# A four-layer kernel on one core: another order for the parts of all five engines, and PSUM banks taken from a table

## The reference, cut to what matters

```
x = x + attn0(xn, 16 heads, causal, alibi) + rms_norm(silu(xn @ G0) * (xn @ U0)) @ D0   # G0, U0, D0 ternary
x = x + recurrence1(xn) + experts1(xn, top 2 of 16, at most 128 rows each) + shared1(xn)
x = x + softmax((xn @ Wq) @ (xn @ Wk).T / 16) @ (xn @ Wv) @ Wo + (silu(xn @ G2) * (xn @ U2)) @ D2   # spline weights
x = x + attn3(xn, 16 heads, rotary) + (xn + shared3(xn) + experts3(xn, top 2 of 8, bf16))
```

## Time and profile before

| | |
|---|---|
| Median of 3 runs | 1509.37 us (1507.64 to 1509.67) |
| Span of the profiled execution, first to last instruction | 1501.9 us |
| Time around the span, by the median | 7.5 us |
| Instructions | 19,793 |
| Mean granted TensorE clock | 0.908 |
| HBM read, written | 44.03 MB, 10.52 MB |

### The profile page before, as it was taken

The page is one execution under the profiler, slowest core; times in us unless marked ns, Lnnn a source line. Parts: engine busy times, 40 slices in busy tenths (PEclk is TensorE's granted clock), DMA queues, the critical chain, the costliest instruction groups (busy, mean ns, idle before and its releaser), DMA issues.

```text
span 1501.9 us, 19793 instructions
## 1 busy us (share of the span) xinstructions
PE 1244.3 (83%) x7757; PEld 809.6 (54%) x7772; DVE 976.6 (65%) x1840; ACT 668.8 (45%) x967; POOL 420.9 (28%) x402
## 2 busy tenths in 40 slices
PE   0579999999998695889568999997887888788887
PEld 0358776667654352445246988874335345335333
DVE  6986457666648999974488345378546676756660
ACT  3344554655566664543114134231661553463462
POOL 3464440033003133121564123241222301401300
PEclk9979989999999897999569999997889899989988
DMA  7000000002210000044441000004001000100100
GB/s 226 23 1 1 1 2 2 1 2 92 87 46 29 0 29 28 1 138 140 149 67 28 1 1 1 8 18 105 1 1 57 1 0 21 37 1 1 57 0 15
DMA packets 31437, 53.26 MB, mean 35 GB/s; under 512 B 4880, under 2 KB 19440, under 8 KB 30576
## 3 DMA queue, kind: packets, MB, share of 16 engines
q1 hardware_dynamic: 27264, 41.02, 8.7%
q0 software_dynamic: 4080, 10.97, 3.4%
HBM read 44.03 MB, written 10.52 MB: 36 GB/s over the span
## 4 chain that ended last, share of the span: by engine, by line
PE 33%; DVE 22%; issue 6%; ACT 5%; POOL 2%; DMA 1%; SPq 0%; DVEq 0%; POOLq 0%
PE pair L617 11%; PE bank L617 11%; DVE max L1113 4%; PE bank L705 3%; ACT probs L1620 3%; PE pair L673 2%; PE pair L693 2%; POOL inbox L1967 1%; DVE conv L1194 1%; PE pair L655 1%; DVE xn L1032 1%; DVE sin L1081 1%; DVE x L1412 1%; DVE normed L1286 1%; DVE mix_h L1517 1%
## 5 line engine op out<-in xcount | busy, mean ns | idle before, releaser
L1113 DVE TENSOR_REDUCE max<-pair 128x2 f32<-128x1024 f32 (+3 forms) x256 | 250.8, 1019 | 90.4 <-PE pair L673 54.5
L1620 ACT ACTIVATE probs<-pair 128x1024 f32<-128x1024 f32 (+3 forms) x256 | 208.7, 871 | 106.0 <-PE pair L663 65.7
L673 PE MATMUL pair<-ks,qs 50*128 50x512 f32 (+3 forms) x512 | 115.9, 484 | 36.5 <-DVE max L1113 17.4
L705 PE MATMUL bank<-probs,v 128*32 128x512 f32 (+3 forms) x1024 | 127.3, 572 | 5.0 <-ACT probs L1620 4.8
L693 PE MATMUL pair<-qs,ks 52*128 52x512 f32 (+3 forms) x512 | 104.3, 454 | 24.9 <-DVE max L1113 4.5
L1933 POOL TENSOR_TENSOR h_low<-hidden,h_high 128x512 fp32r<-128x512 f32 x64 | 82.4, 1291 | 151.9 <-ACT h_high L1655 151.8
L693 PEld LDWEIGHTS pair<-qs,ks 52*128 52x128 f32 x512 | 47.9, 197 | 109.0 <-issue 36.0
L673 PEld LDWEIGHTS pair<-ks,qs 50*128 50x128 f32 x512 | 53.4, 210 | 88.9 <-DVE max L1113 35.2
L1993 POOL TENSOR_TENSOR h<-mix_h,h 128x512 bf16<-128x512 f32 x48 | 55.4, 1165 | 149.9 <-DVE mix_h L1517 108.5
L1146 DVE TENSOR_TENSOR x<-bank,x 128x512 f32<-128x512 f32 x32 | 22.0, 689 | 105.7 <-PE bank L617 102.2
L1163 DVE SCALAR_TENSOR_TENSOR hidden<-hidden,pair 128x512 f32<-128x512 f32 x64 | 43.8, 684 | 62.8 <-ACT hidden L1647 62.8
(11 more groups left out here) (334 smaller groups left out, 3002.1 us busy)
## 6 DMA issues: line engine op xcount, KB each, us to landing
expert_in<-in_experts_in SPq DMA_DIRECT2D x16, 352.0 KB, 4.1
expert_out<-in_experts_out SPq DMA_DIRECT2D x16, 256.0 KB, 4.9
h<-comb SPq DMA_DIRECT2D x4, 1024.0 KB, 5.8
x<-in_x SPq DMA_DIRECT2D x4, 512.0 KB, 8.2
tern_raw<-in_ffn_in SPq DMA_DIRECT2D x8, 256.0 KB, 6.3
inbox<-zeros SPq DMA_DIRECT2D x4, 512.0 KB, 5.2
tokens<-inbox SPq DMA_DIRECT2D x16, 128.0 KB, 2.3
outbox<-expert_y SPq DMA_DIRECT2D x16, 128.0 KB, 3.4
```

Source lines behind the costliest of these rows:

```text
L673: made = mm(to[:, hh, 0:n], m.qs[g % 2][r0:r0 + AUG + 2, p, qt * P:(qt + 1) * P], m.ks[g % 2][r0:r0 + AUG + 2, p, 0:n], start=True, stop=k ...
L705: made = mm(to[32 * j:32 * j + 32, q0:T], m.v[b % 2][:, kt, G * g + j, :], m.probs[(2 * kt + j // 2) % 4][:, j % 2, q0:T], start=kt == 0, ...
L1113: V.tensor_reduce(m.max[:, g % 2, qt, 2 * p:2 * p + 2], to[:, :, 0:n], AX.X, ALU.max).then_inc(*s.done("top"))
L1620: A.activation(m.probs[(2 * kt + p) % 4][:, :, q0:T], to[:, :, q0:T], ACT.Exp, scale=0.25).then_inc(*s.done("exp"))
```

## The change

`DUE` is replaced for all five engines: every part gets another number. The parts, their instructions and their waits for data and buffers stay as they are. On PE a part moves by 3.6 places on average (35 at most), on DVE by 9.7 (129), on ACT by 2.2 (59), on POOL by 4.9 (62), on SP by 3.3 (16). The number at place n of a name's line belongs to the n-th part of that name. The SP names of `load` are, in this order: ident, x0, bias0, qkv0, x1, x2, x3, extra0, wo0, inbox, small1, vec1, front1, gates1, rest1, qkv2, small3, bias3, qkv3, wo3, shared3.

The rotation of the banks is replaced by `TAKEN`, a table that gives for every PE part its first bank. A part that took a pair still takes one of the same three, and one that took a single bank takes 6 or 7; `weigh` and the parts that had bank 7 for themselves now share both. The waits for a bank's last readers are set as before, for the user that the table gives.

```diff
...
-    "tern_scaled": "4 11 6 8 16 14 15 27 18 29 33 30",
+    "tern_scaled": "5 8 12 11 13 15 16 21 19 20 27 24",
...
-    "stat": "2 1 3 5 13 22 21 24 23 45 25 50 47 48 49 51 161 160 156 163 217 218 223 224 298 300 302 304 346 344 345 347 524 534 533 540 543 554 555 558 570 562 563 572 587 585 586 592 606 607 610 611 636 637 642 643 670 671 666 673 722 723 697 724",
+    "stat": "2 1 3 4 36 38 37 39 71 61 68 72 74 93 104 106 171 172 213 220 224 235 233 251 296 309 321 326 359 379 362 394 525 533 528 534 561 559 555 562 587 594 593 601 597 596 595 600 628 629 622 654 651 652 642 662 688 687 689 690 778 771 774 833",
...
-    "norm": "7 10 12 9 41 44 42 38 57 55 54 56 81 78 79 80 168 169 167 166 231 236 235 232 361 375 360 363 393 391 389 392 547 548 549 546 566 568 569 567 584 577 582 583 601 603 599 600 630 633 631 629 662 661 659 663 694 690 692 691 781 780 778 779",
+    "norm": "7 6 9 10 41 42 48 45 91 83 94 86 195 207 186 120 240 227 237 244 320 262 322 306 350 353 347 355 405 404 406 409 538 539 536 537 566 572 573 567 605 604 606 611 635 636 641 631 655 656 664 676 679 683 670 743 821 764 785 766 893 880 894 896",
...
-    "split_high": "1 499 589",
+    "split_high": "5 558 588",
...
-    "split_low": "2 161 199",
+    "split_low": "8 183 193",
...
-    "based": "8 24 30 41 173 184 196 221",
+    "based": "5 56 61 103 190 216 235 280",
...
-    "load": "1 7 6 0 5 2 8 4 9 17 23 24 33 34 35 76 3 81 82 83 84",
+    "load": "1 2 10 9 15 6 18 13 21 22 23 29 28 32 33 78 19 81 82 85 83",
...
-    "tern_load": "11 13 12 10 14 15 16 18 21 19 20 22",
+    "tern_load": "0 3 5 4 8 7 12 11 14 16 17 20",
...
-    "spline_load": "78 77 79 80",
+    "spline_load": "76 77 79 80",
...
-PLACES = {"pair": ((0, 1), (2, 3), (4, 5)), "acc": ((6,),), "one": ((7,),), "two": ((6,), (7,))}
 BANKS = {"tern_sum": "pair", "turn": "pair", "qkv": "pair", "fold": "pair", "score": "pair", "refold": "pair", "prob": "pair", "weigh": "acc", "back": "one",
          "rows": "pair", "unit": "pair", "down": "one", "mean": "one", "proj": "pair", "gate": "two", "gamma": "pair", "inflow_turn": "pair", "mem_turn": "two",
          "shared": "pair", "count": "two", "expert_turn": "two", "expert_in": "pair", "expert_fold": "two", "expert_out": "two",
@@ -307,11 +306,46 @@
          "mix": "pair"}
 
 
-def bank_ring(name, key):
-    if name == "out":
-        return "one" if key[0] in HEADS else "two"
-    return BANKS[name]
-
+def width(name, key):
+    return 2 if BANKS.get(name) == "pair" else 1
+
+
+
+TAKEN = {name: [int(bank) for bank in banks] for name, banks in {
...
+    "turn": "0040004240020004",
...
+    "weigh": "66667777666677777777666677776666777777776666777766667777666666667777666677776666777766667777666677776666777766667777666677776666",
+    "back": "77766766666767676776777676766676",
...
+    "out": "67667776676777767677767776767676",
...
+    "gamma": "2024",
...
+    "shared": "2040204242242400",
...
+}.items()}
 
 
 FREED = {
@@ -385,14 +419,9 @@
         self.pe, self.dve, self.act, self.pool, self.sp = (
             Engine(e, self.sem(n)) for e, n in ((nc.tensor, "pe_step"), (nc.vector, "dve_step"), (nc.scalar, "act_step"), (nc.gpsimd, "pool_step"), (nc.sync, "sp_step")))
         self.banks, held = {}, {}
-        rank = {}
+        first = {(name, key): bank for name, banks in TAKEN.items() for key, bank in zip(parts["PE"][name], banks)}
         for name, key in self.turns.order["PE"]:
-            ring = PLACES[bank_ring(name, key)]
-            n = rank.get(bank_ring(name, key), 0)
-            rank[bank_ring(name, key)] = n + 1
-            place = ring[n % len(ring)] if name != "weigh" or key[-1] == 0 else self.banks["weigh", key[:-1] + (0,)][0]
-            if name == "weigh" and key[-1] > 0:
-                rank[bank_ring(name, key)] = n
+            place = tuple(range(first[name, key], first[name, key] + width(name, key)))
             self.banks[name, key] = (place, [held[bank] for bank in place if bank in held])
             for bank in place:
                 held[bank] = (name, key)
```

More of the change, by code:

```diff
@@ L307 @@
          "mix": "pair"}
-def bank_ring(name, key):
-    if name == "out":
-        return "one" if key[0] in HEADS else "two"
-    return BANKS[name]
+def width(name, key):
+    return 2 if BANKS.get(name) == "pair" else 1
+TAKEN = {name: [int(bank) for bank in banks] for name, banks in {
+    "tern_sum": "024022442024",
+    "turn": "0040004240020004",
+    "qkv": "00402022240402444204400200422424",
+    "fold": "2020424204420402040442242442000200244040222004222004240242242440",
+    "score": "4224440242220402022444002044200242004042404440224440000024040442220440004420220440040424204244204024042240004404020044420042224024040042422002402442220022004402402000200402444042242004404220244422444240224004242440040224222024440002440244200204242402022442",
+    "refold": "42220222220004224000400220442042",
+    "prob": "4400402024042440204222400044042240200240222424240240200202422424240404204422202404422002404022024242222440424042024404402004400444020442000442402404204204222204224242044200004242042020440420420240024242020240404040000220420242200042422002042400040402044202",
+    "weigh": "66667777666677777777666677776666777777776666777766667777666666667777666677776666777766667777666677776666777766667777666677776666",
+    "back": "77766766666767676776777676766676",
+    "rows": "202424402204",
+    "out": "67667776676777767677767776767676",
+    "unit": "0224404020440420200404204002400240200442024240240424020420400224",
+    "down": "76676677",
+    "mean": "6766",
+    "proj": "4204244022422224",
+    "gate": "6767776666677667",
+    "gamma": "2024",
+    "inflow_turn": "4420",
+    "mem_turn": "76777676",
+    "shared": "2040204242242400",
+    "count": "6667",
+    "merge": "76",
+    "expert_turn": "7676777777667667",
+    "expert_in": "4020044240240442",
+    "expert_fold": "6667676776677666",
+    "expert_out": "6667766767767766",
+    "spline": "240420402042",
+    "qk2": "2024",
+    "v2": "76767676",
+    "score2": "6766667667666676",
+    "probs_turn": "7767767667777676",
+    "comb_turn": "6767",
+    "mix": "202024224424444224400204244000022200044020240244",
+}.items()}
 FREED = {
```

## The result

The changed kernel takes **1366.1 us** by the median of four executions, the kernel before 1508.5 us: ratio 0.907, 95% interval 0.903 to 0.911. One of the four executions of the changed kernel took 2456.2 us, for a reason that no trace shows; it counts in the median of 1366.1 but not in the ratio, and the other three have a median of 1363.5 us. The profiled execution has a span of 1362.2 us against 1501.9 before, 139.7 less.

A forecast was written before the change was run, and what follows sets the result against it. PE was busy 1244.3 of 1501.9 us, leaving 257.6 idle to win, with DVE chains in places. Terms -20 - 8 - 12 - 5 - 4 + 8 = -41 gave 1461, plus 7.5 around the span 1468 us; 8-in-10 range 1446 to 1498.

The forecast's parts named there:

- Part 1: Start, 0 to 130 us: earlier loads and a shorter DVE list start dense PE work 15.7 to 23.9 us sooner; 20 taken.
- the cover: Stats and norms put off from the start fit into DVE's 134 us idle in 130 to 450; otherwise 5.9 us cost.
- rival (a): Only the start is gained, later lists just shuffle waits: 1489 us, from 1484 to 1503; chance 0.22.
- Part 2: Layer 1, 450 to 711 us: turn(1,3) loses its 9.7 us bank wait, six table loads go; -8, between +5 and -15.
- Part 3: Layer 1 to 2, 711 to 779 us: earlier spline load, less DVE work ahead of cut_low(2,0); -12, at most 16.5.
- Part 4: Layer 2 to 3, 985 to 1060 us: first probabilities start while DVE works on group 1; -5, between 0 and -12.
- Part 5: Bank table elsewhere, 1060 to 1502 us: longer reuses of pairs save waits, shorter give back; -4, between -13 and +13.
- rival (b): Slower through short bank reuse in score and prob runs of layers 0 and 3: 1524 to 1553 us; chance 0.07.
- New waits: Reordered lists make waits of their own in the two dense stretches, 22.5 us idle PE: +8, between 0 and +22.
- PE busy time: Whole kernel: PE's busy time was expected to stay within 1% of 1244 us.
- The 7.5 us around the span: Median 1509.4 less profiled span 1501.9, taken as untouched time around the span and added to 1461, giving 1468.

The follow-up runs named there:

- start_new: Kernel before, with only the parts starting before 122.9 us in the new order with the new table: 1498.7 us, ratio 0.998.
- start_new_free: As start_new, but the 89 parts wanting a pair between 80 and 215 us take the one free first in start_new's trace: 1492.5 us, ratio 0.993.
- old_order_banks: Kernel before in its old order, but each part takes the bank or pair that came free first in its trace: 1490.7 us, ratio 0.989.
- order_rotation: Changed kernel's new order on all engines, but banks by the old rotation except for 32 parts: 1460.5 us, ratio 0.972.
- l3_rotation: As layer3_new, but last-layer pairs and single banks go by the old rule except for 8 parts: 1470.8 us, ratio 0.978.
- l3_singles_rotation: As layer3_new, but last-layer single banks go by the old rule except for seven parts; pairs stay: 1439.6 us, ratio 0.958.
- layer3_new: Kernel before, with only the last layer in the new order with its table: 1429.9 us, ratio 0.949.
- l3_pairs_rotation: As layer3_new, but last-layer pairs go by the old rotation again; single banks stay as in the table: 1463.2 us, ratio 0.975.
- l3_early_norms: As layer3_new, but last-layer stats and norms of batches 1 to 3, with roots and adds, stand in their old place: 1441.7 us, ratio 0.959.

## Why the prediction was wrong, point by point

**Part 1, the start: right as far as it went.** 20 forecast, 26.5 measured at unit(0,0,7). Timeline of the start, kernel after (start, length, instruction, idle before):

```profile
3.74 0.62 ACT L1567 CAST tern_w<-tern_raw 128x512 bf16<-128x512 f32 x1 [1.72 <-DMA tern_raw<-in_ffn_in]
...
8.76 0.39 DVE L1041 BATCH_NORM_STATS2 stats<-x 128x6 f32<-128x256 f32 x1
...
11.77 0.69 DVE L1012 TENSOR_SCALAR tern_scale<-pair 128x512 bf16<-128x512 f32 x1 [0.54 <-PE pair L657]
...
35.12 0.79 PE L646 MATMUL pair<-wqk_high,cut_high 128*128 128x512 f32 x1 [0.52 <-DVE cut_low L1074]
```

The stats start at 8.76 without the 7.82 us for x, tern_scaled(0) at 11.77 with 0.54 instead of 4.25 us of waiting, and the first wqk product starts at 35.12, inside the 30 to 37 that I named. What failed is the cover: "land in 130 to 450, where DVE has 134 us idle". It holds only with the new list behind it and its table. Alone, the start is worth 0.2% (start_new) to 0.7% (start_new_free), which is also what became of rival (a) at 1489.

**Part 2, layer 1: right in size, its named cause worth little.** 8 forecast, 7.3 measured. turn(1,3) has lost its wait:

```profile
521.76 1.09 PE L665 MATMUL pair<-ident_r,xn 128*128 128x128 f32 x8
```

Its lead is 61.8 us, 15.5 more than at out(0,3,1), and at mem_turn(3,0) 43.7 are left. In old_order_banks, where nothing but banks changed, turn(1,3) gains 10.2 us over out(0,3,1) (4.7, then 14.9) and count(3) has 4.0 again. So this wait on PE was no step of the path. What bounds the stage instead, DVE as I had written beside it, no run tested, and what makes the 7.3 was not taken apart. The Trainium skill (ScalarE: Activation LUTs, What ACT_TABLE_LOAD costs) would have made six loads less worth 16 us and this part up to 15; it came out at half of that, with the loads at the same 1283 ns, and no run isolates them. ACT's table loads are 38, as counted; the largest group is unchanged from the earlier trace rows:

```profile
L1763 ACT ACT_TABLE_LOAD x8 | 10.3, 1283 | 0.1
```

**Part 3, layer 1 to 2: right.** 12 forecast, 13.9 measured. order_rotation has it too (0.7 at out(1,3,0), 16.7 at turn(2,0)), so it is the order's. The first cubic and the first spline product of the kernel after:

```profile
673.24 0.69 DVE L1449 TENSOR_TENSOR cubics<-spline_points,spline_q 96x512 f32<-96x512 f32 x1 [10.34 <-DMA spline_mask<-in_spline_crossed]
...
673.99 2.10 PE L915 MATMUL pair<-cubics,powers 16*128 16x512 f32 x6 [7.58 <-DVE cubics L1449]
```

PE waits 7.6 us here instead of 13.53.

**Part 4, layer 2 to 3: undersized**, 5 forecast, 14.3 measured, just beyond its bound of 12.

**Part 5, the banks: this is the step that failed.** The forecast had 4 us, at most 13. I counted after how many other units a pair is asked for again, found 188 sooner against 157 later, and took "their share, 18% of 70 us". The distance in units is not what PE waits for; it waits for the last reader of that pair, and a reader of another chain (mixed, gated, cut_low) may stand far back in DVE's list. I had written exactly this against rival (b), "the rotation often stands behind the slow holder while another pair is free", and had read one such case, but I did not count them: 56 us of 122 us of bank waits in the trace of before.

The sum failed in two more places. For the last layer I had no term of the order at all, and l3_rotation shows 34 us there for the order with the old rotation. And I added order and banks as if they were independent: 44 and 14 us apart are 142 together, and the 84 us had no term. That my order terms (-20 - 8 - 12 - 5 + 8 = -37) are close to the 44 us of order_rotation is luck: by its trace the start's gain is gone by the end of layer 0 (-1.4 us, where my terms have 12 left), and 22.6 of its 50.7 us come in the last layer, where I had none.

**New waits: wrong in sign.** +8 forecast; the two dense stretches had 22.5 us of idle PE before and have 7.6 now. Under the rotation the sign would have been right and the size too small: order_rotation falls from 25.3 us at unit(0,0,7) to -1.4 at refold(0,3,3).

**PE busy time: the missing term.** "PE busy within 1% of 1244": it is 1214.3, 2.4% less. I treated busy time as fixed because the instructions are, with a clock of 0.90 in the last layer in front of me. That is 30.0 of the 98.7 us by which the span beat the forecast's 41. What moves the clock stays open.

**The 7.5 us around the span.** The sum adds the median less the profiled span, as if 7.5 us lay around the span. In all executions whose span is known, time and span differ by 1.25 to 2.5 us (1363.54 against 1362.2 in the profiled one of the changed kernel); the rest of the 7.5 was the difference between one execution and the median. It shifts the forecast by some 6 us and explains little of the miss.

**The rivals.** (b) asked for at least 0.22 us lost at each of 188 short reuses; the tops' share of the scores' waits fell from 17.4 to 5.9 us. No loss of that kind shows; what a short reuse costs by itself was not run.

## What to carry to other kernels

An engine that runs in order and takes its buffers by rotation waits for the reader of the next place in turn, however late it is. Count from the trace how often another place was free by then: it tells where a table of places can act, and a run must tell what it gives (here 52 of 56 us of such waits gone for 9 us of span). A new order and a new allocation are not to be priced one after the other: 44 and 14 us apart were 142 together. And where the granted clock is below full in a stretch, PE's busy time is not a constant of the sum: 30 of the 140 us of the span were the same matmuls in less busy time, and of the 80 us of span that came only with both changes it was 49.

## What the runs showed of the hardware

The granted clock does not simply rise as PE idles less. In the last layer under the old order, 68.5 us of idle time went with a clock of 0.89 and 51.5 with 0.88 (52.3 with 0.87 in the second such kernel). Under the new order, 48.4 went with 0.92, 44.0 with 0.94 and 26.5 with 0.96. Which pattern of waits decides this was not tried.

The clock also differs without any change to the work: the stretch from refold(0,3,3) to turn(1,3), the same instructions in the same order, took 152.7 us at 0.89 in the kernel before and in l3_singles_rotation, and 156.2 us at 0.85 in layer3_new, l3_pairs_rotation and l3_early_norms. The old last layer took 430.0 to 439.7 us in six traces. Differences of 4 us over 150, or of 9 over 440, between two single traces therefore prove nothing.
